# Paired products of 512 columns (hi*hi and hi*lo of the first half side by side) and the ranks first in each chunk, in a conditioned LoRA feed-forward kernel

## The chip, the cores and the metric

The kernel runs on one core of a Trainium2 chip. The metric is the device time of one execution in microseconds (us). The engines named below are PE (TensorE: products), DVE (VectorE), ACT (ScalarE), POOL (GpSimd) and SP (SyncE, which issues DMAs). Each has its own instruction queue and runs it in order; they meet at semaphores.

## The reference, cut to what matters

```python
def ref(x, cond, cond_w, W_base, b_base, W_gate, A, B):   # x: (64, 32, 512)
    W = cond_w[cond]                                # (64, 32, 32)
    y = einsum('bct,bcd->bdt', x, W)                # mix the 32 channels of each batch
    result = y @ W_base.T + b_base                  # 512 -> 512
    logits = y @ W_gate.T                           # 8 experts
    route_w = normalised top-2 of softmax(logits)
    h = einsum('bnd,erd->bner', y, A)               # 8 experts x 16 ranks = 128 ranks
    delta = einsum('bner,eor->bno', h * route_w[..., None], B)
    return x + result + delta
```

All of it is fp32.

## The kernel before, in words

The 64 x 32 rows are 16 tiles of 128 rows (4 batches each). `mix_tile(t)` multiplies a tile of `x` with a block-diagonal matrix `mix` and leaves `y` transposed in `y_ps`. To keep fp32 accuracy with the faster fp32r products, each operand is split into a high and a low part: `y_hi` by ACT (`split_y`), `y_lo` = `y` - `y_hi` by DVE (`low_y`), and in the same way the weights (`w_hi`, `w_lo`), the LoRA matrix (`b_hi`, `b_lo`) and the routed ranks (`hwT_hi`, `hwT_lo`). A product is then three: hi*hi, hi*lo and lo*hi.

The weights `w_all` have 648 columns: first half of the base (256, `BASE`), 64 ranks, second half of the base (256), 64 ranks, 8 logits. The contraction runs over 512 features in 4 chunks (`c`), so the main sum of a tile has 12 steps (`ORDER`: chunk by chunk, three products each). `main_step` issues each step as two products, one of 320 columns into bank 0 of `main_ps[t % 2]` and one of 328 columns into bank 1. In the last two tiles (`TAIL`, 14 and 15) the steps are cut differently: `side_step` does the 392 columns behind the first 256 (ranks, second base half, logits) and `base_step` the first 256, so that ranks and logits of a tile are complete before its base.

When the main sum of tile t is complete (`main_done`), DVE runs `route_tile(t)`: maximum, its index, one-hot, weight (with one exponential on ACT), and `hw`, the weighted ranks. PE transposes `hw` (`turn`), ACT and DVE split it (`split_hwT`, `low_hwT`), PE adds the LoRA part to the base sums of the same tile (`lora`, 6 products of 256 columns), and DVE adds the sums to `x_sb` (`finish`), to which `add_bias` has added the bias before; SP stores the tile.

The order on each engine is written out by hand. On PE a middle tile t (1 to 13) is: `mix_tile(t + 1)`, a wait for `y_lo_ready` and for `result_ready` of tile t-2 (whose banks tile t takes), four steps, `turn(t - 1)`, five steps, `lora(t - 1)`, three steps. In tile 14 the turn of tile 13 stands before side step 6 (`TAIL_TURN_AT[0]`) and `lora(13)` behind the last side step. On DVE the turn of work of tile t is `route_tile(t - 1)`, `select(t + 2)` (the `mix` matrix), `low_hwT(t - 1)`, `low_y(t + 1)`, `add_bias`, `finish(t - 1)`. `add_bias` comes once in most tiles, twice in tiles 12 and 13. The line numbers of the profile: L505 `mix_tile`, L518 `main_step`, L528 `turn`, L534 `lora`, L591 `side_step`, L597 `base_step`, L630 the last LoRA part, L390 to L408 `route_tile`, L417 `low_hwT`, L383 `low_y`, L424 `add_bias`, L428 `finish`, L486 the last two additions.

Of the kernel before, what the change touches and what calls it, by code (L numbers as in the profile page):

```python
# [5 lines left out]
def adaln_ffn_kernel(  # L6
# [7 lines left out]
    out: bass.AP,  # L14
):


# [5 lines left out]
    f32r = mybir.dt.float32r  # L23
# [3 lines left out]
    ALU = mybir.AluOpType  # L27
# [32 lines left out]

    TAIL_TURN_AT = 6, 9, 6
    PICKED = 2
# [9 lines left out]
    with ctx:  # L72
        def sb(name, shape, dt=f32):
            return ctx.enter_context(nc.sbuf_tensor(name, shape, dt))
# [12 lines left out]
        b_hi = sb("b_hi", [P, OUT], f32r)  # L87
        b_lo = sb("b_lo", [P, OUT], f32r)
        bias_sb = sb("bias_sb", [P, OUT])
# [89 lines left out]
        hwT_hi_ready = sem("hwT_hi_ready")  # L179
        hwT_lo_ready = sem("hwT_lo_ready")  # L180
        base_done = sem("base_done")
        result_ready = sem("result_ready")
        stored = sem("stored")

        def side_sums(t):

            return main_ps[t % 2][:, 1, 0:SIDE]

        def base_sums(t):

            return [main_ps[t % 2][:, 0, 0:BASE], main_ps[t % 2][:, 1, H:H + BASE]]

        def two_runs(of, step, count):
            first = of[:, 0:count]
            return bass.AP(first.tensor, first.offset, [first.ap[0], [step, 2], [1, count]])

        def first_halves():
# [81 lines left out]
        def _(act):  # L279
# [46 lines left out]
        def _(dve):  # L326
# [58 lines left out]

            def route_tile(t, h, logits):
                dve.wait_ge(main_done, t + 1)
# [55 lines left out]

            def route_tail(t):
                side = side_sums(t)
                route_tile(t, two_runs(side, H + BASE, H), side[:, SIDE - E:SIDE])

            for t in range(1, LAST):
                before = main_ps[(t - 1) % 2]
                route_tile(t - 1, before[:, :, BASE:HALF], before[:, 1, HALF:HALF + E])  # L450
# [11 lines left out]
                if t < LAST - 2:  # L462
                    add_bias(t - 1)
# [7 lines left out]
                dve.wait_ge(base_done, t)  # L471
                dve.wait_ge(xb_ready, t)
                finish(t - 1, before[:, :, 0:BASE])

            route_tail(LAST - 1)
            low_hwT(LAST - 1)
            route_tail(LAST)
            dve.wait_ge(base_done, LAST)
            dve.wait_ge(xb_ready, TILES)

            finish(LAST - 1, two_runs(main_ps[(LAST - 1) % 2].ap().rearrange("p h n -> p (h n)"), 512 + H, BASE))
            low_hwT(LAST)
# [7 lines left out]
        def _(pe):  # L490
# [19 lines left out]
            def operands(c, n, t):  # L510
                y, w = ((y_hi, w_hi), (y_hi, w_lo), (y_lo, w_hi))[n]
                return y[t % 2][:, c * P:(c + 1) * P], w[:, c, :]

            def main_step(t, i, c, n):
                y, w = operands(c, n, t)
                for half in range(2):
                    n_cols = HALF + half * E
                    last = pe.matmul(main_ps[t % 2][:, half, 0:n_cols], y,  # L518
                                     w[:, half * HALF:half * HALF + n_cols],
                                     start=i == 0, stop=i == STEPS - 1)  # L520
                if i == STEPS - 1:
                    last.then_inc(main_done, 1)

            def turn(t):
# [4 lines left out]

            def lora(t, sums):  # L530
                pe.wait_ge(hwT_lo_ready, t + 1)
                for n, (h, w) in enumerate(((hwT_hi, b_hi), (hwT_hi, b_lo), (hwT_lo, b_hi))):
                    for half in range(2):
                        last = pe.matmul(sums[half], h[t % 2][:, :],  # L534
                                         w[:, half * BASE:(half + 1) * BASE],
                                         start=False, stop=n == 2, skip_group_check=True)
                last.then_inc(base_done, 1)
# [30 lines left out]
            for t in range(1, LAST - 1):  # L568
                if t > 1:
                    mix_tile(t + 1)  # L570
                if t == 1:
                    pe.wait_ge(y_hi_ready, 2)
                else:
                    pe.wait_ge(y_lo_ready, t + 1)
                    pe.wait_ge(result_ready, t - 1)
                for i, (c, n) in enumerate(ORDER):
                    if t == 1 and (c, n) == (0, 2):
                        pe.wait_ge(y_lo_ready, 2)
                    if i == SECOND_MIX_AT and t == 1:
                        mix_tile(2)  # L580
                    if i == TURN_AT:
                        turn(t - 1)
                    if i == LORA_AT:
                        if t == 1:
                            pe.wait_ge(b_lo_ready, 1)
                        lora(t - 1, [main_ps[(t - 1) % 2][:, half, 0:BASE] for half in range(2)])
                    main_step(t, i, c, n)

            def side_step(t, i):
                y, w = operands(*ORDER[i], t)  # L590
                last = pe.matmul(side_sums(t), y, w[:, BASE:ALL], start=i == 0, stop=i == STEPS - 1)  # L591
                if i == STEPS - 1:
                    last.then_inc(main_done, 1)

            def base_step(t, i):
                y, w = operands(*ORDER[i], t)
                pe.matmul(base_sums(t)[0], y, w[:, 0:BASE], start=i == 0, stop=i == STEPS - 1)  # L597

# [5 lines left out]
            for i in range(STEPS):  # L604
                if i == TAIL_TURN_AT[0]:
                    turn(one - 1)
                side_step(one, i)
            lora(one - 1, [main_ps[(one - 1) % 2][:, half, 0:BASE] for half in range(2)])
            for i in range(STEPS_BETWEEN):
# [7 lines left out]
            for i in range(STEPS_BETWEEN, STEPS):  # L617
                base_step(one, i)
            lora(one, base_sums(one))
            for i in range(STEPS):  # L620
# [4 lines left out]
            for half in (1, 0):  # L625
                n = slice(half * BASE, (half + 1) * BASE)
                for k, (h, w) in enumerate(((hwT_hi, b_hi), (hwT_hi, b_lo), (hwT_lo, b_hi))):
                    if half == 1 and k == 2:
                        pe.wait_ge(hwT_lo_ready, TILES)
                    last = pe.matmul(base_sums(two)[half], h[two % 2][:, :], w[:, n], start=False, stop=k == 2,  # L630
                                     skip_group_check=True)
                last.then_inc(base_done, 1)

# [34 lines left out]
```

## Time and profile before

| What | Value |
| --- | --- |
| median of 3 runs | 95.29 us (95.18 to 96.72) |
| the profiled execution's own time | 95.55 us |
| its span (first to last instruction) | 93.7 us |
| PE busy | 89.8 us, 96% |
| DVE busy | 65.4 us, 70% |
| ACT busy | 23.8 us, 25% |
| share of the last chain on PE | 91% |
| instructions on PE: products and weight loads | 640 and 640 |

The profile is of one execution. "Busy" is the time in which an engine works on some instruction. A product's record lasts longer than its share of the engine, because products overlap: what one costs in a stream is the distance between the starts. PEld is PE's weight load, which runs beside the product before it. The chain that ended last is followed back from the last instruction, at each step to what released it.

### The profile page before, as it was taken

How to read it: one execution, taken by the hardware profiler on the slowest of the kernel's cores; microseconds unless marked ns; L12 is line 12 of the kernel's file. 1: busy time of each engine (PE TensorE's matmuls, PEld its weight loads, DVE VectorE, ACT ScalarE, POOL GpSimd, SP SyncE). 2: the span in 40 equal slices, each digit the busy share in tenths (PEclk: the TensorE clock that was granted, in tenths of full speed). 3: DMA queues.
4: the chain of work that ended last, by engine and by line, in shares of the span. 5: the costliest groups of instructions: out<-in, count | busy, mean ns of one | idle time of the engine just before them, and what ended most of it. 6: DMA issues, size and time to landing. Idle time of an engine off the chain costs nothing.

```text
span 93.7 us, 1810 instructions
## 1 busy us (share of the span) xinstructions
PE 89.8 (96%) x640; PEld 86.6 (92%) x640; DVE 65.4 (70%) x232; ACT 23.8 (25%) x56; POOL 16.7 (18%) x29
## 2 busy tenths in 40 slices
PE   6899999999999999999999999999999999999980
PEld 2289999999999999999999999999999999999970
DVE  2598987867675767867675767867675968867660
ACT  5148721312213040312213040312213031311210
POOL 5148503210304040210404040210400000000000
PEclk9999999999999999999999999999999999999999
DMA  1999094422407061421507061331607020302023
GB/s 37 290 367 354 18 190 160 149 86 80 150 0 229 2 199 38 147 84 73 158 0 227 11 195 36 115 119 62 174 5 224 0 112 0 111 8 112 0 112 112
DMA packets 6360, 10.65 MB, mean 114 GB/s; under 512 B 1008, under 2 KB 1616, under 8 KB 6352
## 3 DMA queue, kind: packets, MB, share of 16 engines
q1 hardware_dynamic: 5760, 10.25, 34.5%
q0 software_dynamic: 448, 0.23, 1.1%
q8 instruction: 5, 0.08, 0.3%
q10 hardware_dynamic: 144, 0.07, 0.2%
q14 instruction: 3, 0.02, 0.1%
HBM read 6.35 MB, written 4.19 MB: 112 GB/s over the span
## 4 chain that ended last, share of the span: by engine, by line
PE 91%; DVE 3%; DMA 3%; issue 0%; DVEq 0%
PE main_ps L518 53%; PE y_ps L505 15%; PE main_ps L534 11%; PE main_ps L591 5%; PE main_ps L597 3%; DMA cond_sb<-cond 3%; PE hwT_ps L528 2%; DVE pick L344 2%; DVE x_sb L486 1%; PE hwT_ps L505 0%; PE main_ps L630 0%; DVE mix L367 0%; DVE mixw L359 0%; PE main_ps L541 0%; DVE own_cond L336 0%
## 5 line engine op out<-in xcount | busy, mean ns | idle before, releaser
L518 PE MATMUL main_ps<-w_lo,y_hi 128*128 128x320 f32 x112 | 26.8, 321 | 0.0
L518 PE MATMUL main_ps<-w_hi,y_hi 128*128 128x320 f32 x112 | 26.8, 320 | 0.0
L518 PE MATMUL main_ps<-w_hi,y_lo 128*128 128x320 f32 x112 | 25.8, 311 | 0.0
L259 POOL DMA_INDIRECT mixw<-cond_w,row_ids x14 | 13.8, 985 | 47.2 <-PE y_ps L505 45.3
L518 PEld LDWEIGHTS main_ps<-w_hi,y_lo 128*128 128x128 f32 x112 | 19.0, 188 | 0.0
L518 PEld LDWEIGHTS main_ps<-w_lo,y_hi 128*128 128x128 f32 x112 | 18.5, 189 | 0.1
L518 PEld LDWEIGHTS main_ps<-w_hi,y_hi 128*128 128x128 f32 x112 | 18.1, 190 | 0.0
L505 PE MATMUL y_ps<-mix,x_sb 128*128 128x128 f32 x124 | 16.6, 276 | 0.2 <-DVE mix L367 0.2
L505 PEld LDWEIGHTS y_ps<-mix,x_sb 128*128 128x128 f32 x124 | 15.6, 191 | 0.4 <-DVE mix L367 0.4
L292 ACT ACTIVATE second<-top 128x1 f32<-128x1 f32 x16 | 4.7, 295 | 42.8 <-DVE top L390 42.8
L417 DVE TENSOR_TENSOR hwT_lo<-hwT_ps,hwT_hi 128x128 fp32r<-128x128 f32 x16 | 4.7, 292 | 13.0 <-ACT hwT_hi L299 13.0
L428 DVE TENSOR_TENSOR x_sb<-main_ps,x_sb 128x512 f32<-128x512 f32 x15 | 10.4, 690 | 4.8 <-PE main_ps L534 4.7
L424 DVE TENSOR_TENSOR x_sb<-x_sb,bias_sb 128x512 f32<-128x512 f32 x16 | 10.8, 683 | 0.0
L288 ACT ACTIVATE y_hi<-y_ps 128x512 fp32r<-128x512 f32 x15 | 9.0, 597 | 6.5 <-PE y_ps L505 6.5
L383 DVE TENSOR_TENSOR y_lo<-y_ps,y_hi 128x512 fp32r<-128x512 f32 x15 | 10.2, 682 | 0.1
L299 ACT ACTIVATE hwT_hi<-hwT_ps 128x128 fp32r<-128x128 f32 x16 | 4.4, 277 | 12.1 <-issue 7.0
L534 PE MATMUL main_ps<-b_hi,hwT_lo 128*128 128x256 f32 x30 | 6.0, 283 | 0.0
L408 DVE SCALAR_TENSOR_TENSOR hw<-main_ps,weight,route 128x128 f32<-128x128 f32 x16 | 5.6, 351 | 0.6
L534 PE MATMUL main_ps<-b_lo,hwT_hi 128*128 128x256 f32 x30 | 6.0, 282 | 0.0
L534 PE MATMUL main_ps<-b_hi,hwT_hi 128*128 128x256 f32 x30 | 6.0, 281 | 0.0
L534 PEld LDWEIGHTS main_ps<-b_hi,hwT_hi 128*128 128x128 f32 x30 | 5.1, 188 | 0.0
L367 DVE TENSOR_TENSOR mix<-mixw,diag_mask 128x128 f32<-128x128 f32 x16 | 4.5, 284 | 0.2
(66 smaller groups left out, 87.3 us busy)
## 6 DMA issues: line engine op xcount, KB each, us to landing
x_sb<-x SPq DMA_DIRECT2D x16, 256.0 KB, 2.8
out<-x_sb SPq DMA_DIRECT2D x15, 256.0 KB
w_raw<-w_all SPq DMA_DIRECT2D x4, 324.0 KB, 3.3
b_raw<-b_lora SPq DMA_DIRECT2D x1, 256.0 KB
bias_sb<-bias SPq DMA_DIRECT2D x1, 256.0 KB
out<-x_sb SPq DMA_DIRECT2D x2, 128.0 KB
mixw<-cond_w,row_ids POOLq DMA_INDIRECT x14, 2.5
table<-cond_w ACTq DMA_DIRECT2D x1, 64.0 KB, 2.6
```

The source lines that it names most:

```text
L259: pool.indirect_dma_start(mixw[:, t, :], None, cond_w, bass.IndirectOffsetOnAxis(row_ids[:, t:t + 1], 0))\
L288: act.activation(y_hi[t % 2][:, :], y_ps[t % 2][:, :], ACT.Copy).then_inc(y_hi_ready, 1)
L292: act.activation(second[:, :], top[:, 0:1], ACT.Exp, bias=top[:, 1:2], scale=-1.0)\
L383: dve.tensor_tensor(y_lo[t % 2][:, :], y_ps[t % 2][:, :], y_hi[t % 2][:, :].bitcast(f32), ALU.subtract).then_inc(y_lo_ready, 1)
L408: dve.scalar_tensor_tensor(out=hw[t % 2][:, :].rearrange("p (h e r) -> p h e r", h=2, e=G), in0=h.rearrange("p h (e r) -> p h e r", e=G), ...
L417: dve.tensor_tensor(hwT_lo[t % 2][:, :], hwT_ps[t % 2][:, 0:P], hwT_hi[t % 2][:, :].bitcast(f32), ALU.subtract).then_inc(hwT_lo_ready, 1)
L424: dve.tensor_tensor(x_sb[:, t, :], x_sb[:, t, :], bias_sb[:, :], ALU.add).then_inc(xb_ready, 1)
L428: dve.tensor_tensor(tile, sums, tile, ALU.add).then_inc(result_ready, 1)
L505: last = pe.matmul(dst, x_sb[:, t, f], mix[t % 2][:, :, :], start=True, stop=True)
L518: last = pe.matmul(main_ps[t % 2][:, half, 0:n_cols], y, w[:, half * HALF:half * HALF + n_cols], start=i == 0, stop=i == STEPS - 1)
L534: last = pe.matmul(sums[half], h[t % 2][:, :], w[:, half * BASE:(half + 1) * BASE], start=False, stop=n == 2, skip_group_check=True)
L591: last = pe.matmul(side_sums(t), y, w[:, BASE:ALL], start=i == 0, stop=i == STEPS - 1)
```

## The change

Weights and LoRA matrix are kept with high and low part side by side (`w_split`, `b_split`), so that one product can read the high and the low part of the first base half as 512 columns. In tiles 1 to 13 (`PAIRED`) each chunk now has three `side_step` products of 392 columns, then one of 512 (`paired_step`: `y_hi` with the high and the low part) and one of 256 (`y_lo` with the high part). The 512 columns fill bank 0: hi*hi in its first half and hi*lo in its second, so the low part is a sum of its own. `finish` adds it to `x_sb` with one more DVE operation of 256 columns, which waits for `first_half_done`; the operation of 512 columns that follows waits for `low_part_added` and `base_done`. `lora` does its first half in the same way, one product of 512 and one of 256 columns, then the second half. Tile 0 keeps 24 products, cut at 256 and 392 columns. The turn stands behind the side products of chunk 1, the LoRA part behind chunk 2. In tile 14 the turn stands before side step 4 in place of 6, and `lora(13)` before side step 9 in place of behind step 11. On DVE `add_bias(t - 1)` is moved ahead of `low_hwT` in tiles 2 to 12. `split_y` no longer waits for `main_done`.

```diff
+    PAIRED = range(1, LAST - 1)
-    TURN_AT, LORA_AT = 4, 9
-    SECOND_MIX_AT = 4
+    TURN_IN, LORA_BEHIND = 1, 2
-    TAIL_TURN_AT = 6, 9, 6
+    TAIL_TURN_AT = 4, 9, 6
+    TAIL_LORA_AT = 9
...
-        w_hi = sb("w_hi", [P, CHUNKS, ALL], f32r)
-        w_lo = sb("w_lo", [P, CHUNKS, ALL], f32r)
+        w_split = sb("w_split", [P, CHUNKS, 2, ALL], f32r)
+        w_hi, w_lo = w_split[:, :, 0, :], w_split[:, :, 1, :]
...
+        def paired_sums(t):
+            return main_ps[t % 2][:, 0, 0:2 * BASE]
...
             def split_y(t):
                 act.wait_ge(y_done, t + 1)
-                if t >= 2:
-                    act.wait_ge(main_done, t - 1)
...
-            def finish(t, sums):
+            def finish(t):
                 tile = x_sb[:, t, :].rearrange("p (h n) -> p h n", h=2)
-                dve.tensor_tensor(tile, sums, tile, ALU.add).then_inc(result_ready, 1)
+                if t in PAIRED:
+                    dve.wait_ge(first_half_done, t)
+                    dve.tensor_tensor(tile[:, 0, :], paired_sums(t)[:, BASE:2 * BASE], tile[:, 0, :], ALU.add)\
+                        .then_inc(low_part_added, 1)
+                    dve.wait_ge(low_part_added, t)
+                dve.wait_ge(base_done, t + 1)
+                dve.tensor_tensor(tile, both_base_sums(t), tile, ALU.add).then_inc(result_ready, 1)
...
+                if 1 < t < LAST - 2:
+                    add_bias(t - 1)
                 if t < LAST - 1:
                     low_hwT(t - 1)
                     low_y(t + 1)
...
+            def paired_step(t, c, low):
+                f = slice(c * P, (c + 1) * P)
+                if low:
+                    pe.matmul(base_sums(t)[0], y_lo[t % 2][:, f], w_hi[:, c, 0:BASE], start=False,
+                              stop=c == CHUNKS - 1)
+                else:
+                    pe.matmul(paired_sums(t), y_hi[t % 2][:, f], w_split[:, c, :, 0:BASE], start=c == 0, stop=False)
...
+                if t in PAIRED:
+                    pe.matmul(paired_sums(t), hwT_hi[t % 2][:, :], b_split[:, :, 0:BASE],
+                              start=False, stop=False, skip_group_check=True)
...
+                last = lora_step(t, 2, 0)
+                if t in PAIRED:
+                    last.then_inc(first_half_done, 1)
+                for n in range(3):
+                    last = lora_step(t, n, 1)
                 last.then_inc(base_done, 1)
...
-                for i, (c, n) in enumerate(ORDER):
+                for c in range(CHUNKS):
+                    side_step(t, 3 * c)
+                    side_step(t, 3 * c + 1)
...
+                    side_step(t, 3 * c + 2)
+                    if c == TURN_IN:
+                        if t == 1:
+                            mix_tile(2)
                         turn(t - 1)
+                    paired_step(t, c, False)
+                    paired_step(t, c, True)
+                    if c == LORA_BEHIND:
...
+                        lora(t - 1)
```

What stood on PE in a middle tile (tile 3) from its start to the turn, before the change; the numbers behind the names are those of the buffers:

```order
L505 MATMUL y_ps0<-mix0,x_sb 128x128 x4
L518 MATMUL main_ps1<-w_hi,y_hi1 128x320
L518 MATMUL main_ps1<-w_hi,y_hi1 128x328
L518 MATMUL main_ps1<-w_lo,y_hi1 128x320
L518 MATMUL main_ps1<-w_lo,y_hi1 128x328
L518 MATMUL main_ps1<-w_hi,y_lo1 128x320
L518 MATMUL main_ps1<-w_hi,y_lo1 128x328
L518 MATMUL main_ps1<-w_hi,y_hi1 128x320
L518 MATMUL main_ps1<-w_hi,y_hi1 128x328
L528 MATMUL hwT_ps0<-ident,hw0 128x128
```

The same stretch of the changed kernel, from the mix to the turn and the pair behind it:

```order
L520 MATMUL y_ps0<-mix0,x_sb 128x128 x4
L538 MATMUL main_ps1<-w_split,y_hi1 128x392 x2
L538 MATMUL main_ps1<-w_split,y_lo1 128x392
L552 MATMUL main_ps1<-w_split,y_hi1 128x512
L549 MATMUL main_ps1<-w_split,y_lo1 128x256
L538 MATMUL main_ps1<-w_split,y_hi1 128x392 x2
L538 MATMUL main_ps1<-w_split,y_lo1 128x392
L558 MATMUL hwT_ps0<-ident,hw0 128x128
L552 MATMUL main_ps1<-w_split,y_hi1 128x512
L549 MATMUL main_ps1<-w_split,y_lo1 128x256
```

The turn stands behind six products of 392, one of 512 and one of 256 columns, where it stood behind four of 320 and four of 328.

On DVE, the end of the work of tile 13 and the router of tile 13 behind it, before:

```order
L417 TENSOR_TENSOR hwT_lo0<-hwT_ps0,hwT_hi0 128x128
L383 TENSOR_TENSOR y_lo0<-y_ps0,y_hi0 128x512
L424 TENSOR_TENSOR x_sb<-x_sb,bias_sb 128x512 x2
L428 TENSOR_TENSOR x_sb<-main_ps0,x_sb 128x512
L390 MAX top<-main_ps1 128x8
```

And in the changed kernel:

```order
L432 TENSOR_TENSOR hwT_lo0<-hwT_ps0,hwT_hi0 128x128
L396 TENSOR_TENSOR y_lo0<-y_ps0,y_hi0 128x512
L439 TENSOR_TENSOR x_sb<-x_sb,bias_sb 128x512 x2
L445 TENSOR_TENSOR x_sb<-main_ps0,x_sb 128x256
L449 TENSOR_TENSOR x_sb<-main_ps0,x_sb 128x512
L405 MAX top<-main_ps1 128x8
```

Between the two `add_bias` and the router one operation of 256 columns has come in.

On PE the start of tile 14 in the changed kernel:

```order
L520 MATMUL y_ps1<-mix1,x_sb 128x128 x4
L538 MATMUL main_ps0<-w_split,y_hi0 128x392 x2
L538 MATMUL main_ps0<-w_split,y_lo0 128x392
L538 MATMUL main_ps0<-w_split,y_hi0 128x392
L558 MATMUL hwT_ps1<-ident,hw1 128x128
L538 MATMUL main_ps0<-w_split,y_hi0 128x392
L538 MATMUL main_ps0<-w_split,y_lo0 128x392
L538 MATMUL main_ps0<-w_split,y_hi0 128x392 x2
L538 MATMUL main_ps0<-w_split,y_lo0 128x392
L568 MATMUL main_ps1<-b_split,hwT_hi1 128x512
L562 MATMUL main_ps1<-b_split,hwT_lo1 128x256
```

Four side products stand ahead of the turn and five between it and the LoRA part; before, six stood at either place.

## Rows read from the trace of the kernel before

**Rows 1.** The page: busy shares, PE's granted clock by slices, chain by engine.
```profile
PE 89.8 (96%) x640; PEld 86.6 (92%) x640; DVE 65.4 (70%) x232; ACT 23.8 (25%) x56; POOL 16.7 (18%) x29
PEclk9999999999999999999999999999999999999999
PE 91%; DVE 3%; DMA 3%; issue 0%; DVEq 0%
```

**Rows 2.** The chain that ended last, in time order: start us, us, what.
```profile
16.93 0.89 PE y_ps L505 x8
17.83 1.19 PE main_ps L518 x8
19.01 0.11 PE hwT_ps L528
19.12 1.49 PE main_ps L518 x10
20.61 0.71 PE main_ps L534 x6
21.32 0.90 PE main_ps L518 x6
...
80.38 0.89 PE y_ps L505 x8
81.27 1.07 PE main_ps L591 x6
...
84.22 0.95 PE main_ps L597 x8
```

**Rows 3.** PE's timeline, last base product of the first group, side products of tile 15.
```profile
84.89 0.28 PE L597 MATMUL main_ps<-w_lo,y_hi 128*128 128x256 f32 x1
...
85.36 0.34 PE L591 MATMUL main_ps<-w_lo,y_hi 128*128 128x392 f32 x1
...
86.59 0.34 PE L591 MATMUL main_ps<-w_hi,y_lo 128*128 128x392 f32 x1
```

**Rows 4.** Timeline of all engines, a middle tile: turn, its split.
```profile
50.57 0.27 PE L528 MATMUL hwT_ps<-ident,hw 128*128 128x128 f32 x1
...
50.88 0.28 ACT L299 ACTIVATE hwT_hi<-hwT_ps 128x128 fp32r<-128x128 f32 x1 [0.70 <-issue]
51.19 0.29 DVE L417 TENSOR_TENSOR hwT_lo<-hwT_ps,hwT_hi 128x128 fp32r<-128x128 f32 x1 [0.91 <-ACT hwT_hi L299]
```

**Rows 5.** DVE's timeline, end of tile 13 and router of tile 13.
```profile
77.83 0.68 DVE L383 TENSOR_TENSOR y_lo<-y_ps,y_hi 128x512 fp32r<-128x512 f32 x1
78.42 1.28 DVE L424 TENSOR_TENSOR x_sb<-x_sb,bias_sb 128x512 f32<-128x512 f32 x2
79.63 0.68 DVE L428 TENSOR_TENSOR x_sb<-main_ps,x_sb 128x512 f32<-128x512 f32 x1
80.41 0.17 DVE L390 MAX8 top<-main_ps 128x8 f32<-128x8 f32 x1
...
81.44 0.35 DVE L408 SCALAR_TENSOR_TENSOR hw<-main_ps,weight,route 128x128 f32<-128x128 f32 x1
```

**Rows 6.** Timelines of PE's weight loads (PEld) and of PE, start of tile 14.
```profile
80.99 0.19 PEld L591 LDWEIGHTS main_ps<-w_hi,y_hi 128*128 128x128 f32 x1
...
82.00 0.14 PEld L528 LDWEIGHTS hwT_ps<-ident,hw 128*128 128x128 f32 x1
...
81.02 0.42 PE L591 MATMUL main_ps<-w_hi,y_hi 128*128 128x392 f32 x1
81.28 0.34 PE L591 MATMUL main_ps<-w_lo,y_hi 128*128 128x392 f32 x1
...
82.17 0.27 PE L528 MATMUL hwT_ps<-ident,hw 128*128 128x128 f32 x1
```

**Rows 7.** Line 486, the two DVE additions of 256 columns: duration ns min/median/max.
```profile
L486 DVE TENSOR_TENSOR x_sb<-main_ps,x_sb x2: 425/425/425, 90.7 to 91.1; 128x256 f32<-128x256 f32 x2
```

More of the change, by code:

```diff
@@ L180, in adaln_ffn_kernel @@
         hwT_lo_ready = sem("hwT_lo_ready")
+        first_half_done = sem("first_half_done")
+        low_part_added = sem("low_part_added")
         base_done = sem("base_done")
@@ L384, in low_y, with route_tile @@
                                   ALU.subtract).then_inc(y_lo_ready, 1)
-            def route_tile(t, h, logits):
+            def route_tile(t):
+                side = side_sums(t)
+                h, logits = two_runs(side, H + BASE, H), side[:, SIDE - E:SIDE]
                 dve.wait_ge(main_done, t + 1)
@@ L442, in _ @@
             dve.wait_ge(experts_ready, 1)
-            def route_tail(t):
-                side = side_sums(t)
-                route_tile(t, two_runs(side, H + BASE, H), side[:, SIDE - E:SIDE])
             for t in range(1, LAST):
-                before = main_ps[(t - 1) % 2]
-                route_tile(t - 1, before[:, :, BASE:HALF], before[:, 1, HALF:HALF + E])
+                route_tile(t - 1)
                 if t == 1:
@@ L460, in _ @@
                     low_hwT(t - 1)
-                if t < LAST - 2:
-                    add_bias(t - 1)
+                if t == 1:
+                    add_bias(0)
                 if t == LAST - 3:
@@ L470, in _ @@
                     add_bias(LAST)
-                dve.wait_ge(base_done, t)
                 dve.wait_ge(xb_ready, t)
-                finish(t - 1, before[:, :, 0:BASE])
-            route_tail(LAST - 1)
+                finish(t - 1)
+            route_tile(LAST - 1)
             low_hwT(LAST - 1)
-            route_tail(LAST)
-            dve.wait_ge(base_done, LAST)
+            route_tile(LAST)
             dve.wait_ge(xb_ready, TILES)
-            finish(LAST - 1, two_runs(main_ps[(LAST - 1) % 2].ap().rearrange("p h n -> p (h n)"), 512 + H, BASE))
+            finish(LAST - 1)
             low_hwT(LAST)
@@ L515, in main_step, with side_step, base_step @@
                 y, w = operands(c, n, t)
[L516 to L520, printed above, removed]
+                pe.matmul(base_sums(t)[0], y, w[:, 0:BASE], start=i == 0, stop=i == STEPS - 1)
+                last = pe.matmul(side_sums(t), y, w[:, BASE:ALL], start=i == 0, stop=i == STEPS - 1)
                 if i == STEPS - 1:
                     last.then_inc(main_done, 1)
+            def side_step(t, i):
+                y, w = operands(*ORDER[i], t)
+                last = pe.matmul(side_sums(t), y, w[:, BASE:ALL], start=i == 0, stop=i == STEPS - 1)
+                if i == STEPS - 1:
+                    last.then_inc(main_done, 1)
+            def base_step(t, i):
+                y, w = operands(*ORDER[i], t)
+                pe.matmul(base_sums(t)[0], y, w[:, 0:BASE], start=i == 0, stop=i == STEPS - 1)
+            def paired_step(t, c, low):
[5 more added lines that the diff above has]
+                    pe.matmul(paired_sums(t), y_hi[t % 2][:, f], w_split[:, c, :, 0:BASE], start=c == 0, stop=False)
             def turn(t):
@@ L528, in turn, with lora_step, lora @@
                 pe.transpose(hwT_ps[t % 2][:, 0:P], hw[t % 2][:, :], ident[:, :]).then_inc(hwT_done, 1)
-            def lora(t, sums):
-                pe.wait_ge(hwT_lo_ready, t + 1)
[L532 to L536, printed above, removed]
+            def lora_step(t, n, half):
+                h, w = ((hwT_hi, b_hi), (hwT_hi, b_lo), (hwT_lo, b_hi))[n]
+                return pe.matmul(base_sums(t)[half], h[t % 2][:, :], w[:, half * BASE:(half + 1) * BASE],
+                                 start=False, stop=n == 2, skip_group_check=True)
+            def lora(t):
+                pe.wait_ge(hwT_lo_ready, t + 1)
+                if t in PAIRED:
+                    pe.matmul(paired_sums(t), hwT_hi[t % 2][:, :], b_split[:, :, 0:BASE],
+                              start=False, stop=False, skip_group_check=True)
+                else:
+                    lora_step(t, 0, 0)
+                    lora_step(t, 1, 0)
+                last = lora_step(t, 2, 0)
[3 more added lines that the diff above has]
+                    last = lora_step(t, n, 1)
                 last.then_inc(base_done, 1)
@@ L575, in _ @@
                     pe.wait_ge(result_ready, t - 1)
-                for i, (c, n) in enumerate(ORDER):
-                    if t == 1 and (c, n) == (0, 2):
+                for c in range(CHUNKS):
+                    side_step(t, 3 * c)
+                    side_step(t, 3 * c + 1)
+                    if t == 1 and c == 0:
                         pe.wait_ge(y_lo_ready, 2)
-                    if i == SECOND_MIX_AT and t == 1:
-                        mix_tile(2)
-                    if i == TURN_AT:
+                    side_step(t, 3 * c + 2)
+                    if c == TURN_IN:
+                        if t == 1:
+                            mix_tile(2)
                         turn(t - 1)
-                    if i == LORA_AT:
+                    paired_step(t, c, False)
+                    paired_step(t, c, True)
+                    if c == LORA_BEHIND:
                         if t == 1:
                             pe.wait_ge(b_lo_ready, 1)
[L586 to L597, printed above, removed]
+                        lora(t - 1)
             one, two = TAIL
@@ L606, in _ @@
                     turn(one - 1)
+                if i == TAIL_LORA_AT:
+                    lora(one - 1)
                 side_step(one, i)
-            lora(one - 1, [main_ps[(one - 1) % 2][:, half, 0:BASE] for half in range(2)])
             for i in range(STEPS_BETWEEN):
@@ L618, in _ @@
                 base_step(one, i)
-            lora(one, base_sums(one))
+            lora(one)
             for i in range(STEPS):
@@ L625, in _ @@
             for half in (1, 0):
[L626 to L632, printed above, removed]
+                lora_step(two, 0, half)
+                lora_step(two, 1, half)
+                if half == 1:
+                    pe.wait_ge(hwT_lo_ready, TILES)
+                lora_step(two, 2, half).then_inc(base_done, 1)
 def kernel(**inputs):
```

6 lines of the change are left out of this document (4 added, 2 removed).

## Prediction, made before the changed kernel ran

> **What bounds the kernel now.** I read the busy table and the chain of waits first. TensorE (PE) is busy for 96% of the span, its granted clock is at full speed in every slice, and the chain that ended last lies on it for 91% [rows 1]. In time order that chain is one pattern repeated for every tile: `mix_tile` 0.89 us, 8 products of the main sum 1.19, the turn (the transpose of `hw`) 0.11, 10 products 1.49, the LoRA part 0.71, 6 products 0.90 [rows 2]. From 16.93 to 80.38 there are 12 such periods, 5.29 us each, with no wait inside. So in tiles 1 to 13 only the issue pace of products counts; what VectorE (DVE), ScalarE and the DMAs do is hidden as long as each result arrives before PE asks for it. I then read that spare time, place by place, since the change adds work to DVE.
>
> **The pace of a product.** Every product carries its own weight load, hidden behind the product before it. The price is therefore the distance from one start to the next:
> - 320 or 328 columns (324 on average): 3.58 us for 24, so 0.149 us [rows 2].
> - 256 columns: 0.95 us for 8, so 0.119 us [rows 2].
> - 392 columns: 1.07 us for 6, 0.178 us [rows 2]; 7 distances from 85.36 to 86.59 give 0.176 [rows 3]. I take 0.177.
> - 512 columns of this kind do not occur. From 256 to 392 a column costs (0.177 - 0.119)/136 = 0.43 ns; carried on by 120 columns from 392, this gives 0.228 us. Lower bound: the smallest slope the rows allow, (0.176 - 0.149)/68 = 0.40 ns, from 0.176, gives 0.224. Upper bound: two products of 256, 0.238, that is, fusing brings nothing. I take 0.228, because the three measured sizes lie almost on one line.
>
> **The change in tiles 1 to 13, on PE.** The number of columns does not change: 24 products with 7,776 columns become 12 of 392, 4 of 512 and 4 of 256, again 7,776. Four products fewer are issued. The sum is 12 x 0.177 + 4 x 0.228 + 4 x 0.119 = 3.51 us against 3.58, a gain of 0.07. The LoRA part goes from 6 products (0.71) to one of 512 and four of 256, 0.228 + 0.476 = 0.704, a gain of 0.006. Together about 0.074 us a tile; over 13 tiles 0.96 us. With the bounds of the two unknown prices (0.224 with 392 at 0.176; 0.238 with 392 at 0.178) the gain is 1.4 or 0.2 us. Tile 0 only cuts its pairs elsewhere: 0.119 + 0.177 for 0.298, worth nothing.
>
> The Trainium skill, TensorE: Matmul & The Clock Gate, section "Back-to-back issue gap", gives the warm distance as N/2.4 + 2.5 ns. This speaks against the change: an estimate by it saves 5 x 2.5 ns a tile, 0.16 us in all. The rows disagree with it here, 119 ns for 256 columns where it gives 109 [rows 2].
>
> **DVE in an ordinary tile.** Each paired tile adds one 256-column addition, 0.425 us by the row of that size [rows 7], and the 512-column addition of `finish` then waits for it (`low_part_added`). A hand-over takes 0.04 us, from the end of the turn at 50.84 to ScalarE at 50.88 [rows 4]. Count from the start of the LoRA part. Its first-half sum closes 0.23 (the product of 512) + 0.28 (the record of one of 256 [rows 3]) + 0.04 = 0.55 later, the small addition lasts until 0.98, the large one starts at 1.01 and ends at 1.70 (0.68 long [rows 5]). PE needs that result for the next tile after 0.70 + 3 x 0.177 + 0.347 + 0.89 = 2.47 us: 0.77 to spare. The router of the same tile starts at about 1.62 and delivers `hw` 1.38 later (80.41 to 81.44 + 0.35 [rows 5]), at 3.0; the turn comes at 2.47 + 0.08 + 1.41 = 3.96, where 0.08 is what the first distance behind a `mix_tile` has over 0.177 (81.02 to 81.28 [rows 6]). `hwT_lo` is there 0.95 after the turn (50.57 to 51.19 + 0.29 + 0.04 [rows 4]), the LoRA part asks for it 1.34 after. So additions, router and the moved `add_bias` all stay hidden in tiles 2 to 12. In tile 1 the turn again follows `mix_tile(2)`, and the margins before it grow by the two further products.
>
> **Where the cover is thin: tile 13 into tile 14.** On DVE tile 13 has two `add_bias` between `low_y` and `finish` (78.42 for 1.28 us), and `finish(12)` follows at 79.63 without a wait; the router's first operation for tile 13 starts at 80.41, `hw` is written at 81.79 [rows 5], and the turn's weight load comes at 82.00 [rows 6]. That is only 0.2 us of slack, and the change takes from it three times.
> 1. `low_hwT(12)` starts when the turn in tile 13 is through. The turn moves from behind 8 products (1.19) to behind 6 x 0.177 + 0.228 + 0.119 = 1.41: DVE's row of work is 0.22 later, so `finish(12)` starts at 79.85 on the clock of before.
> 2. The small addition and its hand-over are 0.47: the large one starts at 80.32. Two such operations in a row start 0.605 apart (78.42 to 79.63 for two), so the router starts at 80.93 in place of 80.41. The earlier `main_done` brings nothing there, as DVE isn't free.
> 3. `hw(13)` is then written at 82.31. PE wants it earlier than before: tile 14 starts at 81.02 - 0.07 = 80.95, and the turn stands behind 4 side products instead of 6, so at 82.17 - 81.02 - 0.354 = 0.80 after it, 81.75.
>
> With 0.04 of hand-over and 0.03 from weight load to product (80.99 to 81.02 [rows 6]) the turn can run at 82.38: a stall of 0.63 us. Queued behind the turn on PE are the side products of tile 14, all of whose successors are then late by as much. `result_ready` for `finish(12)` comes at 81.05 and holds the first product of tile 14 by about 0.1 us, which is inside the 0.63, not on top. The LoRA part of tile 13, now behind 5 more side products, asks for `hwT_lo` 1.00 after the turn, and it is there 0.95 after it: just in time. The rest of the tail has the same order as before.
>
> **Sum.** Against the profiled execution's own time of 95.55 us (span 93.7): 95.55 - 0.96 + 0.63 = 95.22. The median of the three runs is 0.26 lower, 95.29, which gives 94.96, say 95.0 us.
>
> **Rivals.**
> - *The tail doesn't stall.* Then only the pace counts: 95.29 - 0.96 = 94.3. For it: 0.52 of the 0.63 comes from two estimates, that the shifted turn moves all of DVE's row and that the large addition can't start under the small one; the profile of before has no two additions tied in this way. Against it: `finish(12)` had no wait ahead of it [rows 5], so every addition ahead of the router shifts it one for one.
> - *The price goes by columns, not by product.* Then 512 columns cost 0.238, the change saves 0.2 to 0.3 us, and the stall stays: 95.29 - 0.25 + 0.63 = 95.7. For it: 256 columns at 0.119 and 324 at 0.149 cost nearly the same per column (0.465 and 0.460 ns). Against it: 392 columns at the price per column of 256 would be 0.182, and the rows show 0.176 to 0.178. The page's rule named above would also land near here.
> - *Slower: the moving operand in two runs.* `w_split[:, c, :, 0:BASE]` is two runs of 256 columns, 648 apart; no product of before reads such an operand. If the jump holds the stream up, each of 65 products (5 a tile) pays. The gain is gone beyond (0.96 - 0.63)/65 = 5 ns each; 20 ns each give 95.0 + 1.3 = 96.3, and over 35 ns the loss passes 2%. For it nothing but its absence from the rows; against it, DVE reads its two runs in `finish` in 0.68 us, as long as the one run of `low_y` (0.68) [rows 5].
>
> **How the numbers follow.** Chances: forecast (94.7 to 95.3) 0.50; no stall (94.0 to 94.6) 0.20; price by columns (95.4 to 95.8) 0.15; two runs slow (over 95.8) 0.08; the rest, such as a 512-column product below my bound without a stall, 0.07. The range 94.0 to 95.8 leaves out the slow case and part of the rest. Two per cent, about what a measurement of this kernel can tell from no change, is 1.9 us: below 93.4 lies only a part of the rest, 0.02; above 97.2 the heavy end of the two-run case, 0.03; within, 0.95.
>
> **What would show it.** In the chain the period falls from 5.29 to about 5.21, with 4 products of 512 about 0.228 apart. In ordinary tiles PE has no idle time. At the turn in tile 14 the wait list shows PE's weight load waiting about 0.6 us for DVE's `hw`, and the router's first operation follows the 512-column addition without a gap. I am wrong if the distance behind a 512-column product is above 0.24, if the period's gain is absent, or if the turn of tile 14 runs without a wait.

## The result, and the profile after

The changed kernel takes 95.78 us (median of 20 runs) against 95.41 us for the kernel before beside it; the ratio is 1.0039 with a 95% interval of 1.002 to 1.0058. It is slower by 0.4%, far inside the 2% band, but on the other side of the forecast of 0.3 us faster. The profiled execution took 95.59 us with a span of 93.8 us.

The page of the changed kernel, the lines that answer to [rows 1]:

```profile
PE 89.8 (96%) x575; PEld 83.1 (89%) x575; DVE 69.7 (74%) x245; ACT 23.7 (25%) x56; POOL 15.8 (17%) x29
PEclk9999999999999999999999999999999999999999
PE 88%; DVE 7%; issue 1%; ACT 0%; DVEq 0%
```

PE issues 65 products fewer (575 for 640) and is busy just as long, 89.8 us. The clock is as it was. What is new is DVE on the last chain: 7% where it had 3%. The chain in time order says where (start us, us, what). First an ordinary period, from one `mix_tile` to the next, which answers to [rows 2]:

```profile
22.02 0.89 PE y_ps L520 x8
22.92 0.54 PE main_ps L538 x3
23.45 0.23 PE main_ps L552
23.80 0.55 PE main_ps L538 x3
...
25.68 0.23 PE main_ps L568
25.91 0.47 PE main_ps L562 x4
...
26.93 0.24 PE main_ps L552
27.28 0.89 PE y_ps L520 x8
...
74.64 0.89 PE y_ps L520 x8
```

From 22.02 to 74.64 there are 10 periods of 5.262 us, without a wait; before it was 5.29. The gain is there, but it is 0.025 us a tile, not the forecast 0.074. Three side products last 0.54 (0.179 each, I had 0.177) and the product of 512 columns 0.23 to 0.24 (0.228). Then the chain in tiles 13 and 14:

```profile
76.96 0.12 PE hwT_ps L558
...
77.10 0.29 ACT hwT_hi L312
...
77.41 0.29 DVE hwT_lo L432
77.70 0.59 DVE y_lo L396
78.30 0.43 DVE x_sb L439
...
79.42 0.43 DVE x_sb L445
...
80.48 0.17 DVE top L405
...
81.50 0.36 DVE hw L423
...
81.91 0.33 PE hwT_ps L558
82.24 0.89 PE main_ps L538 x5
83.13 0.30 PE main_ps L568
83.43 0.47 PE main_ps L562 x4
...
85.37 1.60 PE main_ps L538 x9
```

It leaves PE at the turn in tile 13, runs through ScalarE's split, `low_hwT`, `low_y`, two bias additions, the new small addition and the router, and comes back to PE at the turn in tile 14. This is the stall that the prediction named, in its place. The list of waits of the changed kernel says the same (engine line <- waited for: us, times, longest):

```profile
PEld hwT_ps L558 <- DVE hw L423: 0.6, 1, 0.6
```

One more difference stands near the start, in tile 1 of the same chain:

```profile
12.75 0.89 PE y_ps L520 x8
13.64 0.11 PE hwT_ps L558
...
14.99 0.87 PE main_ps L562 x6
15.86 0.54 PE main_ps L538 x3
```

The LoRA part of tile 0 lasts 0.87 us, where the same six products lasted 0.71 in every tile before [rows 2]: a wait that the prediction did not have.

Cut at the same marks, the two chains give (first group of 8 mix pieces, mix of tile 3, mix of tile 14, end of the last LoRA product):

| Stretch | before | after | difference |
| --- | --- | --- | --- |
| 7.11 to 16.93, 6.77 to 16.75 | 9.82 | 9.98 | +0.16 |
| 11 periods, to 75.09, to 74.64 | 58.16 | 57.89 | -0.27 |
| to the end, 90.69, 90.72 | 15.60 | 16.08 | +0.48 |
| sum | 83.58 | 83.95 | +0.37 |

The sum is the same as the difference of the medians (+0.37), in part by luck. The first stretch holds the loads of weights and differs between executions of the same code: for the changed kernel it took 9.98 us here and 10.03 in the repeat below, and 9.87 and 9.89 in two versions below that have the same code up to there. So its +0.16 shows nothing by itself. The part of it behind the loads, from the mix in tile 1 to that of tile 3, does repeat (4.00 here, 4.01 in the repeat), and the wait is read there. That the span grew by only 0.1 is because the changed kernel's execution began its first mix 0.34 us earlier, at 6.77 for 7.11; ahead of that mark both kernels issue the same work, and it came at 6.63 to 7.20 in the executions of this study.

### The profile page after: what moved, and what is told of

The parts are those of the page before. It is cut to its first block, busy times and chain, and to the rows that moved or that the text cites. A ratio compares the mean times of both kernels' runs of the same rounds, so it can differ in the third digit from the quotient of the medians.

```text
span 93.8 us, 1692 instructions
## 1 busy us (share of the span) xinstructions
PE 89.8 (96%) x575; PEld 83.1 (89%) x575; DVE 69.7 (74%) x245; ACT 23.7 (25%) x56; POOL 15.8 (17%) x29
## 4 chain that ended last, share of the span: by engine, by line
PE 88%; DVE 7%; issue 1%; ACT 0%; DVEq 0%
PE main_ps L538 32%; PE y_ps L520 14%; PE main_ps L552 12%; PE main_ps L562 8%; PE main_ps L549 6%; PE main_ps L544 3%; PE main_ps L568 3%; PE hwT_ps L508 2%; PE main_ps L532 2%; PE hwT_ps L558 2%; DVE pick L357 2%; PE main_ps L531 2%; DVE x_sb L501 1%; DVE x_sb L439 1%; DVE y_lo L396 1%
## 5 line engine op out<-in xcount | busy, mean ns | idle before, releaser
L538 PE MATMUL main_ps<-w_split,y_hi 128*128 128x392 f32 x120 | 32.6, 352 | 0.0
L552 PE MATMUL main_ps<-w_split,y_hi 128*128 128x512 f32 x52 | 21.6, 416 | 0.0
L538 PE MATMUL main_ps<-w_split,y_lo 128*128 128x392 f32 x60 | 20.4, 340 | 0.0
L538 PEld LDWEIGHTS main_ps<-w_split,y_hi 128*128 128x128 f32 x120 | 18.7, 189 | 1.2
L549 PE MATMUL main_ps<-w_split,y_lo 128*128 128x256 f32 x52 | 14.6, 280 | 0.0
L538 PEld LDWEIGHTS main_ps<-w_split,y_lo 128*128 128x128 f32 x60 | 11.3, 188 | 0.0
L552 PEld LDWEIGHTS main_ps<-w_split,y_hi 128*128 128x128 f32 x52 | 9.8, 188 | 0.5
L549 PEld LDWEIGHTS main_ps<-w_split,y_lo 128*128 128x128 f32 x52 | 9.8, 189 | 0.0
L445 DVE TENSOR_TENSOR x_sb<-main_ps,x_sb 128x256 f32<-128x256 f32 x13 | 5.5, 423 | 4.8 <-PE main_ps L562 4.8
L562 PE MATMUL main_ps<-b_split,hwT_lo 128*128 128x256 f32 x32 | 9.0, 282 | 0.0
L562 PE MATMUL main_ps<-b_split,hwT_hi 128*128 128x256 f32 x38 | 7.6, 285 | 0.0
L562 PEld LDWEIGHTS main_ps<-b_split,hwT_hi 128*128 128x128 f32 x38 | 5.8, 189 | 0.8 <-issue 0.2
```

Source lines behind the costliest of these rows:

```text
L445: dve.tensor_tensor(tile[:, 0, :], paired_sums(t)[:, BASE:2 * BASE], tile[:, 0, :], ALU.add)\
L549: pe.matmul(base_sums(t)[0], y_lo[t % 2][:, f], w_hi[:, c, 0:BASE], start=False, stop=c == CHUNKS - 1)
L552: pe.matmul(paired_sums(t), y_hi[t % 2][:, f], w_split[:, c, :, 0:BASE], start=c == 0, stop=False)
L562: return pe.matmul(base_sums(t)[half], h[t % 2][:, :], w[:, half * BASE:(half + 1) * BASE], start=False, stop=n == 2, skip_group_check=True)
```

## The experiments

Theory, read from the two chains: the products' pace gives 0.3 us, and three waits on DVE and PE take more than that back: the turn in tile 14 (0.61), the LoRA part in tile 1 (0.16), the LoRA part of tile 13 (0.06, its 0.77 us against 0.71); the changed tail also removes an older wait at the start of tile 15 (0.17, the 1.77 us below against 1.60 above). Rivals: the loss is in the products (512 columns slow, or two runs slow), or in the new order as a whole.

### One bias addition out of the way

```diff
                 if 1 < t < LAST - 2:
                     add_bias(t - 1)
+                if t == LAST - 2:
+                    add_bias(LAST - 2)
...
                 if t == LAST - 2:
-                    add_bias(LAST - 2)
                     add_bias(LAST - 1)
```

> The changed kernel with one edit on VectorE: in the work of tile 13 the first of the two bias additions stands ahead of low_hwT, where VectorE waits for ScalarE, and no longer ahead of finish. Theory (the loss is in stalls, the largest the turn of tile 14, 0.61 us late by the two chains): finish(12) starts as soon as its first-half sum is closed, hw(13) is there before the turn asks for it, and 0.45 to 0.6 us go (the LoRA part of tile 13 may then wait 0.1 us for hwT_lo). The time falls from 95.8 to about 95.3, about as the kernel before. Rival (the loss is in the pace of the products, or in the change as a whole): no move, 95.8.

Measured: 95.24 us, ratio 0.9974 (0.9944 to 1.0004) to the kernel before. From the mix of tile 14 to the end it takes 15.59 us, against 16.08 in the changed kernel: 0.49 us gone, with the middle unchanged (57.88 for 11 periods). PE's timeline in tile 14, fourth side product, turn, last side product, LoRA part:

```profile
81.38 0.34 PE L539 MATMUL main_ps<-w_split,y_hi 128*128 128x392 f32 x1
81.55 0.28 PE L559 MATMUL hwT_ps<-ident,hw 128*128 128x128 f32 x1
...
82.38 0.34 PE L539 MATMUL main_ps<-w_split,y_lo 128*128 128x392 f32 x1
82.61 0.50 PE L569 MATMUL main_ps<-b_split,hwT_hi 128*128 128x512 f32 x1
82.95 0.28 PE L563 MATMUL main_ps<-b_split,hwT_lo 128*128 128x256 f32 x1
```

The turn follows the fourth side product after 0.17. In the changed kernel it was 0.59:

```profile
81.32 0.34 PE L538 MATMUL main_ps<-w_split,y_hi 128*128 128x392 f32 x1
81.91 0.33 PE L558 MATMUL hwT_ps<-ident,hw 128*128 128x128 f32 x1 [0.25 <-DVE hw L423]
```

One line of order on DVE takes back 0.49 us, more than the 0.37 that the change lost; against the kernel before, the time is not told apart from no change (the interval reaches 1.0004). Not all of the 0.61 comes back, because the next link is short too: the LoRA product of 512 columns now starts 0.23 behind the last side product and holds PE for 0.34, together 0.16 more than in an ordinary tile. The changed kernel already lost 0.06 there, so 0.61 - 0.10 = 0.51 was to be had.

### A dose in the same place

```diff
+        spare = sb("spare", [P, BASE])
...
                     add_bias(LAST)
+                if t == LAST - 2:
+                    dve.tensor_tensor(spare[:, :], bias_sb[:, 0:BASE], bias_sb[:, 0:BASE], ALU.add)
                 dve.wait_ge(xb_ready, t)
                 finish(t - 1)
```

> The changed kernel with one more VectorE operation of 256 columns, into a spare buffer, ahead of finish(12) in the work of tile 13; nothing reads it. Theory: every addition there shifts the router of tile 13 one for one, so the turn of tile 14 is later by what such an operation adds from start to start, about 0.36 us, and so is everything behind it: span and time up by 0.36 us, ratio about 1.007. Rival (VectorE has room there, the wait at the turn is something else): no move.

Measured: ratio 1.0063 (1.004 to 1.0086), 96.07 us. DVE's timeline:

```profile
78.12 1.28 DVE L440 TENSOR_TENSOR x_sb<-x_sb,bias_sb 128x512 f32<-128x512 f32 x2
79.31 0.42 DVE L491 TENSOR_TENSOR spare<-bias_sb 128x256 f32<-128x256 f32 x1
79.65 0.42 DVE L446 TENSOR_TENSOR x_sb<-main_ps,x_sb 128x256 f32<-128x256 f32 x1
80.10 0.69 DVE L450 TENSOR_TENSOR x_sb<-main_ps,x_sb 128x512 f32<-128x512 f32 x1
80.71 0.17 DVE L406 MAX8 top<-main_ps 128x8 f32<-128x8 f32 x1
```

The operation takes 0.34 from start to start, and the stretch from the mix of tile 3 to the end grows by 0.36 against the changed kernel (74.33 for 73.97). One for one: at this place DVE sets the time. The rows also show what the prediction had put at 0.47: the large addition stands 0.45 behind the small one on which it depends (79.65 to 80.10). An independent operation of the same size takes only 0.34 (79.31 to 79.65).

### The second wait

This edit stands on top of the early bias addition.

```diff
-                    if c == LORA_BEHIND:
-                        if t == 1:
-                            pe.wait_ge(b_lo_ready, 1)
-                        lora(t - 1)
+                    if t == 1 and c == LORA_BEHIND + 1:
+                        pe.wait_ge(b_lo_ready, 1)
+                        lora(0)
...
+                    if t > 1 and c == LORA_BEHIND:
+                        lora(t - 1)
```

> As e1_bias_early, and in tile 1 the LoRA part of tile 0 stands behind the side products of chunk 3, not ahead of them, so that hwT_lo(0), which comes 1.3 us after the turn there, has 0.53 us more. Theory of the stalls: the 0.16 us by which the LoRA part of tile 1 is longer than in the other tiles (0.87 against 0.71) goes as well; together 0.65 to 0.75 below the changed kernel, 95.1 us, 0.3 below the kernel before. Rival: the 0.16 is no wait for hwT_lo and stays.

Measured: 95.11 us, ratio 0.9942 (0.9915 to 0.997). From the mix in tile 1 to that of tile 3 it takes 3.87 us (13.31 to 17.18), where the changed kernel takes 4.00 (12.75 to 16.75): 0.13 us. The timeline of this version shows why `hwT_lo` is late: in tile 1 the second mix stands directly ahead of the turn, and ScalarE does `split_y(2)` before it splits `hwT`:

```profile
14.04 0.27 PE L559 MATMUL hwT_ps<-ident,hw 128*128 128x128 f32 x1
14.24 0.60 ACT L301 ACTIVATE y_hi<-y_ps 128x512 fp32r<-128x512 f32 x1 [1.73 <-PE y_ps L521]
14.73 0.27 ACT L312 ACTIVATE hwT_hi<-hwT_ps 128x128 fp32r<-128x128 f32 x1
15.04 0.29 DVE L432 TENSOR_TENSOR hwT_lo<-hwT_ps,hwT_hi 128x128 fp32r<-128x128 f32 x1 [0.85 <-ACT hwT_hi L312]
```

`hwT_lo` is there 1.29 us after the turn's start, not 0.91 as in an ordinary tile. It was 1.29 in tile 1 of the kernel before too, but there the LoRA part came 1.60 us after the turn. This version has the lowest ratio of the study, 0.6% below the kernel before. By the chains, from the mix of tile 3 to the end, it is 73.43 us for 73.76, which is 0.33 us or 0.35%; that lies inside the interval.

### One step too far

> As e2_bias_and_lora, and on VectorE low_hwT(13) stands ahead of low_y(15). In e2 the LoRA part of tile 13 still waits about 0.15 us for hwT_lo, which VectorE does behind low_y at 82.46 although hwT_hi is there at 82.34. Theory: hwT_lo comes 0.08 to 0.1 earlier and the wait shrinks by as much: 95.0 us, 0.1 below e2, about 0.4 below the kernel before. Rival: that wait is not on the last chain, no move.

Its edit on top of the last one is `low_hwT(t - 1)` ahead of `low_y(t + 1)` for tile 14 too. Measured: 94.94 us, ratio 0.9957 (0.9932 to 0.9983), not to be told from the version before it. Its chain gives the stretch from the mix of tile 3 to the end as 73.48 us against 73.43, so nothing is gained, and shows why (its pieces in tiles 14 and 15):

```profile
82.26 0.29 PE main_ps L565
82.55 0.48 PE main_ps L559 x4
83.03 0.54 PE main_ps L535 x3
83.57 0.94 PE main_ps L541 x8
84.51 1.74 PE main_ps L535 x9
```

The LoRA part's first piece shrank from 0.38 to 0.29 as expected, but the first nine side products of tile 15 went from 1.60 to 1.74. DVE did the same work in another order, and with the LoRA part earlier PE now comes to tile 15 before `finish(13)` is through: PE's weight load there starts at 84.37, 0.12 after `finish(13)` ends at 84.25. The expected 95.0 us was met by the median (94.94), but not for the expected reason: it counted one wait and not what is late next.

### The tail as it was

Edit: `TAIL_TURN_AT` is 6, 9, 6 again, and `lora(13)` stands behind the last side step.

> The changed kernel with one part undone: in tile 14 the turn stands before side step 6 again and the LoRA part of tile 13 behind the last side step. Theory of the stalls: of the 0.61 us lost up to that turn, 0.36 go (two side products more stand ahead of it) and 0.15 (tile 14 starts late) plus 0.1 stay; against it the wait of tile 15's first side product for finish(13), 0.17 us long in the kernel before and absent in the changed one, comes back, longer by 0.05 to 0.1 for the second addition. Net 0.1 to 0.2 faster than the changed kernel, 95.6. Rival (place of turn and LoRA part in the tail are well chosen): slower than the changed kernel.

Measured: 95.64 us, ratio 1.0013 (0.9983 to 1.0043); the changed kernel beside it 95.51 and 1.0016 (below). By the chains the stretch from the mix of tile 14 on is 16.02 for 16.08, 0.06 shorter and not 0.1 to 0.2. Its pieces:

```profile
83.64 0.23 PE main_ps L568
83.86 0.47 PE main_ps L562 x4
84.34 0.95 PE main_ps L544 x8
85.28 0.10 issue
85.38 1.85 PE main_ps L538 x9
```

The LoRA part is not waited for (0.23 + 0.47), but the nine side products of tile 15 take 1.85 and stand behind 0.10 of waiting, 1.95 together against 1.60 in the changed kernel. The profile names no releaser for the 0.10 ("issue"), but the semaphore that PE waits for there is that of `finish(13)`, which ends at 85.24. In the kernel before the nine took 1.77, its piece of the chain being:

```profile
85.17 1.77 PE main_ps L591 x9
```

The wait for `finish(13)` is back, 0.35 us where it was 0.17; the expectation had it longer by only 0.05 to 0.1. Ahead of it 0.42 of the changed kernel's 0.67 us of waits in tile 14 are gone. The difference of the two is about the 0.06 measured. So the changed tail is neither gain nor loss; it trades one wait for another of nearly the same size.

### The same wait in the kernel before

```diff
-    TAIL_TURN_AT = 6, 9, 6
+    TAIL_TURN_AT = 5, 9, 6
...
+                if i == 10:
+                    lora(one - 1, ...)
                 side_step(one, i)
-            lora(one - 1, ...)
```

> The kernel before, with the turn of tile 14 before side step 5 (was 6) and the LoRA part of tile 13 before side step 10 (was behind the last). Theory: the 0.17 us by which the first 9 side products of tile 15 last longer in the kernel before (1.77 against 1.60) are a wait for finish(13), and go when the LoRA part starts 0.36 us earlier; the turn finds hw(13) just ready. 0.1 to 0.2 us below the kernel before. Rival: that 0.17 has another cause, no move.

Measured: ratio 0.9985 (0.9961 to 1.0009), so not resolved by the times. By the chain the nine products take 1.59 in place of 1.77: the wait goes, as expected. The LoRA part gets 0.08 longer (0.79), which leaves 0.1 us of gain from the mix of tile 14 to the end. The middle came out 0.08 longer without any edit there, 58.24 for 58.16. A gain of 0.1 us is at the limit of both ways to look.

### The pairs alone

```diff
-    PAIRED = range(1, LAST - 1)
+    PAIRED = range(0)
...
-                    pe.matmul(paired_sums(t), y_hi..., w_split[:, c, :, 0:BASE], start=c == 0, stop=False)
+                    pe.matmul(base_sums(t)[0], y_hi..., w_hi[:, c, 0:BASE], start=c == 0, stop=False)
+                    pe.matmul(base_sums(t)[0], y_hi..., w_lo[:, c, 0:BASE], start=False, stop=False)
```

> The changed kernel without the pairs: the same order of side and base products, but two products of 256 columns in place of each of 512, and finish without its second addition. Theory: a pair saves 0.231 against 2 x 0.119, 7 ns, 5 pairs a tile, so each of 13 tiles is about 0.03 us longer (0.4 us in all by that; 0.2 by the mean distances of the trace), while the missing addition brings the router of tile 13 forward by 0.47 us and takes most of the stall at the turn of tile 14. Net 0 to 0.3 us faster than the changed kernel, 95.5 to 95.8. If the pairs were what costs (a 512-column product slow), it would be clearly faster, below 95.2; if they were the gain forecast (0.07 us a tile), slower by 0.5.

Measured: 95.67 us, ratio 1.002 (0.9986 to 1.0053). 11 periods last 58.18 us for 57.89: the pairs are worth 0.026 us a tile, and without them the new order has the period of the old one (58.18 for 58.16). So the gain in pace comes from the 5 products fewer, and it is 5 ns for each. The stretch from the mix of tile 14 to the end is 15.65 for 16.08, as the router is no longer held up by the second addition. To see the price without the stalls, the same edit on top of the two cures:

> As e2_bias_and_lora (first bias addition of tile 13 early, LoRA part of tile 1 late), without the pairs: two products of 256 in place of each of 512, and finish without its second addition. With the stalls out of the way this is the price of the pairs alone. Theory: the period goes from 5.264 back to 5.290 us as in e3_unpaired, 0.34 us over 13 tiles, and nothing comes back for the missing addition, since VectorE is hidden: 95.4 us, ratio 0.997 to 0.999 to the kernel before against 0.994 for e2. Rival (the pairs are worth nothing, e2's gain is its order alone): the same as e2, 0.994.

Measured: 95.34 us, ratio 0.9995 (0.9968 to 1.0022) against 0.9942 (0.9915 to 0.997) with pairs; the two were not measured beside each other. By the chains, from the mix of tile 3 to the end, 73.79 against 73.43: 0.36 us, 13 tiles at 0.027. With the waits cured the change is the small gain that its pace says; with the waits it is a loss.

### One run or two

> The changed kernel with the 512-column product of the main sum reading one run of columns, w_hi columns 0 to 511, in place of two runs of 256 that lie 648 apart. It computes another sum in the low half (that part of the output is not the reference's); number, size and order of all instructions are the same. Rival of the prediction, the jump between two runs holds the stream up: the distance behind a 512-column product falls from 0.231 us and the time by 52 times that. Theory now: no difference, 0.231 and 95.8 us.

> As e7_swap, with the weights laid out so that the 512 columns of the paired main product are one run: per chunk high rest (392), high first half (256), low first half (256), low rest (392); VectorE's low_w becomes two operations. It computes the whole reference. e6_one_run had a period of 5.247 us in place of 5.264. If the jump between two runs (or where they start) costs, the period falls by 0.02 and the time by 0.2 us against e7_swap, to 94.8; if e6's gain came from its other data or from chance, no difference, 95.0.

The first measured 95.45 us, ratio 0.9995 (0.9967 to 1.0022), and its 11 periods lasted 57.72 us, 0.17 less than in the changed kernel. The second, which computes the reference with one run of 512 columns, measured 95.1 us, ratio 0.9975 (0.9951 to 0.9998), beside 0.9957 for the kernel that it was made from, and its 11 periods lasted 57.96 us for 57.84. So the jump between two runs costs nothing that can be seen. Why the first was 0.015 us a period shorter stays open. Its run starts at the same place as the two runs do, but it reads other data in the second half; as the second version has one run too and is not shorter, the jump alone is not the reason, and data and chance were not separated.

### The changed kernel again

> The changed kernel again, unaltered, beside the others of this call. Both theories: 95.8 us, ratio 1.004 to the kernel before; it says what the other three are to be compared with.

Measured: 95.51 us, ratio 1.0016 (0.9991 to 1.0041); 57.88 us for 11 periods and 16.10 to the end, within 0.02 of the first profile. The expected 1.004 lies in its interval, and so does no change at all: the times alone would not carry the sign of the result, and the first measurement's 1.0039 (1.002 to 1.0058) is the better part of the evidence. The median of the changed kernel moved by 0.3% from one measurement to the next. Marks in the chains repeat to some hundredths where no load is waited for, and to 0.08 us at worst in the middle of the kernel before.

## Why the prediction went wrong, point by point

- **What bounds the kernel**: right. In tiles 2 to 12 PE has no wait, and DVE's second addition, 0.4 us a tile, costs nothing there: the period fell.
- **The pace of a product**: the mechanism was right, the size not. The step that failed is "a gain of 0.07 ... over 13 tiles 0.96 us": it measured 0.025 a tile, 0.32 us. It is a difference of two sums of 3.5 us, and two of the prices that I put in were 1% low. Side products in threes are 0.179 apart, not the 0.177 of [rows 2] and [rows 3], and outside its bounds of 0.176 and 0.178; over 12 that is 0.02 us. The product of 512 columns is 0.231, inside the bounds of 0.224 to 0.238, not 0.228; over 5 that is 0.015. The rest, 0.01, is rounding: the 3.58 us for the 24 products before are three rounded pieces, and the 12 periods give 3.57. The price of 256 columns was right (0.116 to 0.120). Why side products are dearer in threes, and 512 columns dearer than the line through the other sizes, no run here shows. My sum had bounds of 0.2 and 1.4 us for the term, and I took the value "because the three measured sizes lie almost on one line", though the answer hung on the last nanosecond. The lower bound, the rival "the price goes by columns", was nearer: the true gain is only 0.1 us from it.
- **The page's rule**: the Trainium skill, TensorE: Matmul & The Clock Gate, section "Back-to-back issue gap", gives N/2.4 + 2.5 ns for an isolated product. An estimate by it saves 2.5 ns for each product fewer. Measured are 5 ns, between the rule and my 15. For the distances themselves the measurement decides, 231 ns for 512 columns where the rule gives 216.
- **The stall at the turn of tile 14**: right in place, cause and size, 0.63 foretold, 0.61 measured. By PE's timelines tile 14's first product starts 0.96 after the mix, where it was 0.81 (0.15), and what follows the turn is 0.46 late on top. I had the first part at "about 0.1" inside the whole; so it was. It is all hand-over: `finish(12)` ended at 80.56, just when PE would have come, and PE's weight load followed 0.12 later, not the 0.04 that I took from [rows 4]:

```profile
79.87 0.69 DVE L449 TENSOR_TENSOR x_sb<-main_ps,x_sb 128x512 f32<-128x512 f32 x1
...
80.68 0.30 PEld L538 LDWEIGHTS main_ps<-w_split,y_hi 128*128 128x128 f32 x2
```

- **"just in time"** for the LoRA part of tile 13: it waits 0.06 us.
- **Tile 1**: the step that failed is "the margins before it grow". They do ahead of the turn, and I did not look behind it. There the LoRA part comes 1.34 us after the turn instead of 1.60, and `hwT_lo` needs 1.29 and a hand-over, because ScalarE splits `y` first. Both stood in the trace of before, 1.29 and 1.60, with 0.31 us between them. The wait by the chain is 0.16, what the cure gave back 0.13.
- **"The rest of the tail has the same order as before"**: true, but the LoRA part that I had moved forward also frees `finish(13)` earlier, and removes a wait of 0.17 us at tile 15 that I had not noticed in the profile of before (1.77 us for nine side products).
- **The sum**: -0.32 (pace) + 0.61 + 0.06 + 0.16 - 0.17 = +0.34 us, against +0.37 measured. With the forecast 0.96 in place of 0.32 it would have been 0.3 below, which is what I wrote. That is luck in part: the three terms that I did not have cancel to 0.05. The range held the time by 0.02 us; the sign was wrong, by the pace term alone.
- **Two runs slow**: did not happen.

## What to carry to other kernels

Fusing two products into one of the same total width saved 5 ns a product here; if that is the whole gain, measure it in the new sequence or treat the sign as open, because a difference of sums that are 1% uncertain can't carry it. Before adding work to an engine that is hidden on average, look for the one period in which it isn't: here two additions stood ahead of the router in one tile of sixteen, and moving one of them was worth more (0.49 us) than the fused products (0.32). When a wait is cured, ask at once what the moved work meets next; two of the edits here only traded one wait for another.

## What was unexpected of the hardware

- Products of equal columns in the same code differ by a few ns with their neighbours: 392 columns are 0.178 apart in the long run of the tail (1.60 us for nine) and 0.179 in threes between products of 512 and 256 (0.537 on average for three).
- Operations of DVE that don't depend on each other start before the record of the one before ends: 512 columns are 0.69 long and 0.60 apart. One that waits for the result of the one before starts 0.03 after its end (79.42 + 0.42 to 79.87). So a dependent addition of 256 columns put ahead of another costs 0.45 us, not 0.34.
- A PE stream that stood ready was released 0.12 us after the DVE operation that it waited for had ended: 80.56 to 80.68 and 14.76 to 14.88 in the changed kernel, 84.25 to 84.37 in the version with `low_hwT` first. At the turn of tile 14 it was 0.06 (81.85 to 81.91).
